# A decoder layer on one core: context keys transposed in DRAM and split on GpSimd, a new order of the attention loop, expert numbers unpacked with explicit register instructions

## The reference, cut to what matters

```python
x = x + attn(layernorm(x))            # 16 heads of 16, 4 key/value groups, RoPE, causal, window 64 + 4 sink tokens
x = x + xattn(layernorm(x), ctx, ctx) # 16 heads, causal; queries, keys and values are used as they are, no projection
x = x + moe(layernorm(x))             # 16 experts of width 176, top 4 per token, and a shared one of width 704
# xattn: scores = einsum('bhqd,bhkd->bhqk', q, k) / 4, causal mask, softmax, times v
# moe:   coef of the 4 best softmaxed gate logits; h = silu(g) * u; y = h @ w2[e].T, added up with coef
```

## Time and profile before

| | us |
|---|---|
| median of 3 runs | 416.64 |
| lowest, highest | 412.84, 417.04 |
| the profiled execution, as timed | 414.46 |
| its span, first to last instruction | 412.6 |
| busy: PE, weight loads, DVE, ACT, POOL | 364.2, 260.7, 254.8, 180.3, 157.5 |
| mean granted clock of TensorE | 0.960 |

### The profile page before, as it was taken

One profiled execution on the slowest core, in us unless ns is written; L12 is line 12 of the kernel. 1 busy time (PEld: TensorE's weight loads), 2 busy tenths in 40 slices (PEclk: granted clock), 3 DMA queues, 4 the chain that ended last, 5 costly groups with the idle time before them and its releaser, 6 DMA issues.

```text
span 412.6 us, 7763 instructions
## 1 busy us (share of the span) xinstructions
PE 364.2 (88%) x2198; PEld 260.7 (63%) x2198; DVE 254.8 (62%) x744; ACT 180.3 (44%) x538; POOL 157.5 (38%) x203
## 2 busy tenths in 40 slices
PE   7687998989899895986997949999999999999883
PEld 3345675757586864755866725666666666668662
DVE  2647799797979689876254633444444444443894
ACT  1052867676758476674424312333333333332220
POOL 2923416262625324566537500333333333333000
PEclk9898999999989999999798978999999999999997
DMA  7990000878676671111102143667666666662901
GB/s 237 350 387 2 2 1 2 249 221 255 202 251 207 213 247 39 41 67 52 54 26 94 66 143 93 195 191 206 192 202 201 186 208 198 193 195 98 390 24 51
DMA packets 43029, 64.25 MB, mean 156 GB/s; under 512 B 5251, under 2 KB 31892, under 8 KB 42484
## 3 DMA queue, kind: packets, MB, share of 16 engines
q1 hardware_dynamic: 38356, 52.45, 41.0%
q0 software_dynamic: 3792, 10.49, 6.7%
q10 hardware_dynamic: 848, 0.92, 0.9%
HBM read 34.88 MB, written 28.97 MB: 155 GB/s over the span
## 4 chain that ended last, share of the span: by engine, by line
PE 38%; issue 24%; DVE 16%; POOL 13%; ACT 4%; DMA 3%; SPq 1%; POOLq 0%; DVEq 0%
POOL y_picks L595 11%; PE bank L1414 10%; PE bank L1328 5%; PE bank L1343 5%; ACT probs L637 3%; PE bank L1319 3%; DVE neg_max L874 3%; PE bank L1283 3%; PE bank L1314 2%; DVE x L1243 2%; PE bank L1370 2%; PE bank L1302 2%; DVE q_stk L846 1%; PE bank L1397 1%; PE bank L1384 1%
## 5 line engine op out<-in xcount | busy, mean ns | idle before, releaser
L595 POOL DMA_INDIRECT y_picks<-yb,ids x47 | 45.1, 959 | 93.7 <-DVE yb L1215 93.1
L637 ACT ACTIVATE probs<-bank,neg_max 128x128 f32<-128x128 f32 x256 | 69.9, 414 | 16.0 <-DVE neg_max L874 16.0
L1669 PE MATMUL bank<-w,xbt 128*128 x188 | 69.2, 492 | 1.0 <-ACT xbt L764 0.8
L1208 DVE TENSOR_TENSOR hb<-sg,bank 128x176 f32<-128x176 f32 x47 | 15.9, 338 | 67.8 <-issue 23.8
L772 ACT ACTIVATE sg<-bank 128x176 f32<-128x176 f32 x47 | 14.9, 317 | 84.7 <-PE bank L1669 84.7
L1669 PEld LDWEIGHTS bank<-w,xbt 128*128 128x128 f32 x188 | 32.7, 193 | 26.9 <-issue 17.3
L1689 PE MATMUL bank<-w,hbt 128*128 128x256 f32 x188 | 48.2, 380 | 0.0
L874 DVE TENSOR_REDUCE neg_max<-bank 128x4 f32<-128x512 f32 x64 | 41.0, 683 | 11.3 <-PE bank L1319 11.3
L539 POOL DMA_INDIRECT x_slots<-x,slots x32 | 32.8, 1025 | 23.1 <-DVE slots L1003 14.2
L1328 PE MATMUL bank<-ident,probs 128*128 128x128 f32 x256 | 36.6, 282 | 2.1 <-ACT probs L637 2.1
L880 DVE COPY probs_t<-bank 128x512 f32<-128x512 f32 x47 | 31.9, 685 | 7.5 <-PE bank L1328 7.3
(11 more groups left out here) (176 smaller groups left out, 717.0 us busy)
## 6 DMA issues: line engine op xcount, KB each, us to landing
x_slots<-zero_b SPq DMA_DIRECT2D x16, 1056.0 KB, 10.6
w<-w_in_dram SPq DMA_DIRECT2D x47, 256.0 KB
xb<-x_slots SPq DMA_DIRECT2D x47, 132.0 KB, 2.4
w<-w_in_dram SPq DMA_DIRECT2D x4, 1408.0 KB, 10.8
yg<-y_picks SPq DMA_DIRECT2D x8, 512.0 KB, 7.0
sw_raw<-shared_in_dram SPq DMA_DIRECT2D x6, 384.0 KB, 3.5
ctx_sb<-ctx_in_dram SPq DMA_DIRECT2D x1, 1024.0 KB, 12.0
out_dram<-x SPq DMA_DIRECT2D x8, 128.0 KB, 1.8
```

What stands on the lines that cost most here:

```text
L595: pool.indirect_dma_start(y_picks[:, :], bass.IndirectOffsetOnAxis(ids[:, n:n + 1], 0), yb[:, n % RB, :], None).then_inc(yb_placed[n % RB] ...
L637: ins = act.activation(probs[:, g, j, :], ps_s[g][:, 128 * j:128 * j + 128], ACT.Exp, bias=neg_max[:, g, j:j + 1])
L1669: ins = pe.matmul(ps_gu[n % 2][:, 0:GU], xbt[:, n % 2, k, :], w13[:, bass.ds(e, 1), k, :].rearrange("p e n -> p (e n)"), start=k == 0, sto ...
```

## The change

The host lays the context out a second time, with the channel on the partitions: per sequence 128 partitions of 2 x 4 x 128 values, each head's 16 channels written three times and a block of zeros, in the order of the stack. SP loads it, sequence by sequence (512 KB), into `ctxt`. POOL's `split_keys` rounds all of it into `ktc` and then overwrites partitions 32 to 63 and 96 to 127, which hold the low parts and the zeros, with the difference. `stack_context`, `cross_keys` and `cross_k` are gone, and with them `c_stk`, `ctx_rows` and a memset.

The stacks of keys and queries change places: context keys become (high, high, low, 0), context queries (high, low, high, 0).

All four engines' `iteration` is in a new order, `row_max`, `exps` and `transpose_probs` are now called bank by bank, and ACT takes banks 2 and 3 where it took 2. `unpack` writes its two register instructions out.

```diff
@@ SP
+            def load_keys(c):
+                if c:
+                    sp.wait_ge(ktc_ready, 2 * c)
+                sp.dma_start(ctxt[:, :, :, :].rearrange("p u j n -> p (u j n)"), ctxt_in[c]).then_inc(ctxt_loaded, 16)
+            load_keys(0)
+            load_keys(1)
+            load_keys(2)
             sp.wait_ge(zeros_ready, 1)
             for c in range(1, SC):
                 sp.wait_ge(swl_ready, c)
 ...
+                load_keys(c + 2)
@@ POOL
+            def split_keys(c):
+                pool.wait_ge(ctxt_loaded, 16 * c + 16)
+                if not isinstance(c, int) or c:
+                    pool.wait_ge(scores_psum[CROSS], 4 * c)
+                if not isinstance(c, int) or c:
+                    pad_context(c - 1)
+                pool.tensor_copy(ktc[:, :, :, :], ctxt[:, :, :, :]).then_inc(ktc_high, 1)
+                pool.wait_ge(ktc_high, c + 1)
+                for low in (slice(PAD, STK), slice(STK + PAD, 2 * STK)):
+                    pool.tensor_tensor(ktc[low, :, :, :], ctxt[low, :, :, :], ktc[low, :, :, :].bitcast(F32), ALU.subtract
+                                       ).then_inc(ktc_ready, 1)
+                pool.wait_ge(ktc_ready, 2 * c + 2)
             def iteration(t, cross_on, tail_on):
-                if cross_on:
-                    pad_context(t - 1)
+                if tail_on:
+                    split_shared(t - 2)
                 turn(t + 1)
                 if tail_on:
                     inverse_deviation(CROSS, t - 2)
-                stack_context(t)
 ...
+                split_keys(t)
                 if tail_on:
                     keep_rows(t - 2)
-                    split_shared(t - 2)
                 inverse_deviation(SELF, t)
@@ POOL behind the loop, the new order
+            split_shared(SC - 1); inverse_deviation(CROSS, B - 3); split_keys(B - 1); keep_rows(B - 3)
+            inverse_deviation(SELF, B - 1); scatter(0); pad_context(B - 1); inverse_deviation(CROSS, B - 2)
+            keep_rows(B - 2); scatter(1); scatter(2); scatter(3)
@@ PE, iteration, the new order (conditions left out)
+   scores(SELF, t, 0); front_a(t + 1); scores(SELF, t, 1); logits(lot); front_b(t + 1)
+   transpose_probs(SELF, t, 0); transpose_probs(SELF, t, 1); cross_queries(c, 0); turn_values(CROSS, t - 2)
+   transpose_probs(SELF, t, 2); transpose_probs(SELF, t, 3)
+   wait ktc_ready, qtc_ready, probs_t_ready; scores(CROSS, c, 0); cross_queries(c, 1)
+   values(SELF, t, 0); values(SELF, t, 1); scores(CROSS, c, 1); third_norm(t - 2)
+   transpose_probs(CROSS, c, 0); turn_values(SELF, t); transpose_probs(CROSS, c, 1); front_c(t + 1, 0)
+   transpose_probs(CROSS, c, 2); turn_attn(t); transpose_probs(CROSS, c, 3); front_c(t + 1, 1)
+   project(t); values(CROSS, c, 0); values(CROSS, c, 1); ranks(lot)
@@ ACT, iteration, the new order
+   take_values(CROSS, t - 2); front_a(t + 1); exps(SELF, t, 0..3); route_exps(lot); cross_q(c, 0)
+   take_probs_t(SELF, t, 2); take_probs_t(SELF, t, 3); cross_q(c, 1); exps(CROSS, c, 0); take_values(SELF, t)
+   exps(CROSS, c, 1); take_xth(t - 2); exps(CROSS, c, 2); exps(CROSS, c, 3); front_c(t + 1, 0); take_attn_t(t)
+   take_probs_t(CROSS, c, 2); take_probs_t(CROSS, c, 3); front_c(t + 1, 1)
@@ DVE, iteration, the new order
+   second_norm(c); stack_queries(c); row_max(SELF, t, 0..3); route_slots(0) if last; route_shift(lot); front_r(t + 1)
+   first_norms (iterations 0 and 1); take_probs_t(SELF, t, 0); take_probs_t(SELF, t, 1); cross_rows(t - 2)
+   statistics(CROSS, t - 2); row_max(CROSS, c, 0); row_max(CROSS, c, 1); front_p(t + 1); third_norm(t - 2)
+   row_max(CROSS, c, 2); front_l(t + 1); row_max(CROSS, c, 3); take_xtl(t - 2); route_top(lot); normalise(SELF, t)
+   take_probs_t(CROSS, c, 0); front_k(t + 1); take_probs_t(CROSS, c, 1); front_v(t + 1); route_pick(lot)
+   front_n(t + 2); x2 of t; statistics(SELF, t)
@@ PE, expert numbers
             def unpack(n):
-                experts[n] = pe.snap((packed[n // PACK] >> (4 * (n % PACK))) & (NE - 1), min_val=0, max_val=NE - 1)
+                r = pe.alloc_register(f"expert{n}")
+                pe.reg_alu(r, packed[n // PACK], 4 * (n % PACK), ALU.logical_shift_right)
+                pe.reg_alu(r, r, NE - 1, ALU.bitwise_and)
+                experts[n] = pe.snap(r, min_val=0, max_val=NE - 1)
```

More of the change, by code:

```diff
@@ L562, in _ @@
                 iteration(t, True, True)
-            pad_context(B - 2)
+            split_shared(SC - 1)
+            inverse_deviation(CROSS, B - 3)
+            split_keys(B - 1)
+            keep_rows(B - 3)
+            inverse_deviation(SELF, B - 1)
             pool.wait_ge(rows_zeroed, 16 * (NE + 1))
@@ L568, in _ @@
             scatter(0)
[L569 to L573, removed]
             pad_context(B - 1)
-            scatter(2)
             inverse_deviation(CROSS, B - 2)
             keep_rows(B - 2)
+            scatter(1)
+            scatter(2)
             scatter(3)
-            split_shared(SC - 1)
             pool.wait_ge(xn3_kept, B - 1)
@@ L675, in iteration @@
                     take_values(CROSS, t - 2)
+                if not last:
+                    front_a(t + 1)
+                for g in range(TILES):
+                    exps(SELF, t, g)
                 if lot is not None:
                     route_exps(lot)
-                exps(SELF, t, 0)
-                if not last:
-                    front_a(t + 1)
                 if cross_on:
-                    cross_k(t - 1, 0)
                     cross_q(t - 1, 0)
-                exps(SELF, t, 1)
+                take_probs_t(SELF, t, 2)
+                take_probs_t(SELF, t, 3)
                 if cross_on:
-                    cross_k(t - 1, 1)
                     cross_q(t - 1, 1)
-                take_probs_t(SELF, t, 2)
+                    exps(CROSS, t - 1, 0)
                 take_values(SELF, t)
                 if cross_on:
-                    exps(CROSS, t - 1, 0)
+                    exps(CROSS, t - 1, 1)
                 if tail_on:
@@ L1049, in iteration @@
                     front_v(t + 1)
-                if cross_on:
-                    take_probs_t(CROSS, t - 1, 3)
                 if lot is not None:
                     route_pick(lot)
-                if not tail_on:
-                    dve.wait_ge(x_rest, 16)
-                    first_norms(LATER[t])
+                if isinstance(t, int) and t < B - 2:
+                    dve.wait_ge(rstd1_ready, 2)
+                if not isinstance(t, int) or t < B - 2:
+                    front_n(t + 2)
                 dve.wait_ge(wo_psum, t + 1)
@@ L1491, in iteration @@
                     pe.wait_ge(qtc_ready, 2 * t)
-                    pe.wait_ge(ktc_ready, 2 * t)
-                if cross_on:
                     scores(CROSS, c, 1)
+                if lot is not None:
+                    pe.wait_ge(exps_ready, 2 * lot + 2)
+                if last:
+                    pe.wait_ge(slots_ready, 1)
                 if tail_on:
                     third_norm(t - 2, ps_x)
+                if cross_on:
+                    transpose_probs(CROSS, c, 0)
                 turn_values(SELF, t)
+                if cross_on:
+                    transpose_probs(CROSS, c, 1)
                 if not last:
@@ L1501, in iteration @@
                 if cross_on:
[L1502 removed]
+                    transpose_probs(CROSS, c, 2)
                 if tail_on:
@@ L1507, in iteration @@
                 if cross_on:
-                    transpose_probs(CROSS, c, 1)
-                project(t)
-                if lot is not None:
-                    ranks(lot)
+                    transpose_probs(CROSS, c, 3)
                 if not last:
                     front_c(t + 1, 1)
+                project(t)
                 if cross_on:
@@ L1516, in iteration @@
                     values(CROSS, c, 1)
+                if lot is not None:
+                    ranks(lot)
             def count_experts():
@@ L1613, in _ @@
             rows_of(0)
-            transpose_probs(CROSS, B - 1, 0)
-            transpose_probs(CROSS, B - 1, 1)
+            for g in range(TILES):
+                transpose_probs(CROSS, B - 1, g)
             pe.wait_ge(attn_ready[CROSS], B - 1)
```

181 lines of the change are left out of this document (73 added, 108 removed).

## The result

| | before | after |
|---|---|---|
| median, lowest, highest us | 416.84, 412.84, 417.33 | 429.70, 428.41, 430.25 |
| ratio, 95% interval | | 1.0326, 1.0257 to 1.0394 |
| span of the profiled execution | 412.6 | 428.4 |
| mean granted clock | 0.960 | 0.919 |

A forecast was written before the change was run, and what follows sets the result against it. PE and DVE were taken to bound the attention loop together, PE's sequencer the expert loop. Attention -8.9 and experts -8.2 us, together -17.1, take the profiled 414.46 to 397.4; with the median 2.2 above, 399, range 391 to 408.

The forecast's parts named there:

- Expert numbers: Expert loop: shift and mask run under the up matmuls instead of behind a wait; beat 2.50 us, -8.2 us in all.
- POOL's prices: Attention loop, `split_keys` on POOL: cast up to 1.36 us, each subtraction 2.37, whole block with `pad_context` and gaps 7.1.
- the first rival: POOL gates the attention loop; at a block of 9.2 us its gain is gone, about 406 us; chance 0.18.
- the slower rival: POOL's block takes 11.5 us or more, with subtractions of 4.6; beat 23.1, kernel 423 us; chance 0.06.
- the walk through one iteration: One steady attention iteration timed piece by piece from the end of `project`; beat from 20.76 to about 19.2 us.
- stacking 0.85, with POOL now busy beside it 0.4 more: DVE after `second_norm`: stacking takes 0.85 us plus 0.4 for POOL beside it, reaching `row_max(SELF)` at 4.2.
- `front_l` 15.5 (1.34, POOL beside it): DVE after `row_max(CROSS,2)`: `front_l` takes 1.34 us beside POOL and ends at 15.5 us of the iteration.
- the forecast beat: Attention loop: plain beat of about 19.2 us instead of 20.76, -1.55, with POOL nearly co-bound.
- Iterations 6 and 7: Attention loop's end: iteration 6 gains 2.5 us, with PE's mask wait covered; iteration 7 gains half a beat's gain, 0.7.
- The tail: Behind the attention loop: no gain at `scatter(0)`, and `split_keys(7)` may end 0.5 us after the statistics; +0.5 us.
- The start: Iterations 0 and 1: priced at 0, though `split_keys(0)` waits for 512 KB more behind the first loads.
- The wait for the key load that the prediction named at its end: POOL waiting for the key load, named as something that would make the prediction wrong; priced at nothing.

The follow-up runs named there:

- e6: Changed kernel with `front_l(t + 1)` ahead of `row_max(CROSS, t - 1, 2)` on DVE; 410.18 us, ratio 0.9859 to the kernel before.
- e9: e6 with the second norm and `stack_queries` behind the first two SELF row maxima on DVE; 403.36 us, ratio 0.9649 to the kernel before.
- e11: Changed kernel with eight unread matmuls on zeros per beat where PE waits for `k_stk`; 426.38 us, ratio 1.0262 to the kernel before.
- e5: Changed kernel with POOL's `split_shared(t - 2)` moved behind `inverse_deviation(CROSS, t - 2)`; 427.22 us, ratio 1.031 to the kernel before.
- e7: Changed kernel with both the DVE exchange of e6 and the POOL move of e5; 430.25 us, ratio 1.0382 to the kernel before.
- e10: e9 with eight unread matmuls on zeros in iteration 7 and eight in the tail; 404.01 us, ratio 0.9714 to the kernel before.
- e1: Kernel before with only the new `unpack` of the expert numbers; 404.33 us, ratio 0.9749 to the kernel before.
- e4: Changed kernel with both POOL key subtractions cut to 8 columns, so the keys' low part is left out; 407.04 us, ratio 0.9798 to the kernel before.
- e12: e9 with `load_keys(0)` issued on SP ahead of the four loads of `w13`; 405.02 us, ratio 0.9716 to the kernel before.

## Why the prediction was wrong

*Expert numbers: right.* Beat 2.50 in nearly every block, 8.2 us, no ALU_OP at the matmul's line.

*POOL's prices: right.* A subtraction of 1,024 columns on 32 partitions takes 2.37 us, as the slope of rows on 128 partitions gave, so the number of partitions doesn't count; the cast takes 1.04 instead of 1.36, the block 6.3 instead of 7.1. POOL is idle 3.58 us before `rstd`: it doesn't gate the beat, as forecast and against the first rival. At the shorter beats of e6 and e9 this sign turns: there POOL has no idle time before that `rstd`, which starts 0.3 us behind the end of DVE's `ve`. In e6 DVE waits 1.0 us for it (0.8 in after), in e9 it has two row maxima to do first. So POOL is near its limit there, as the prediction said. In the slower rival the place was near, but the mechanism (POOL's subtraction at 4.6 us) was not it.

*The failed step* is the walk through one iteration, at two of its terms: "stacking 0.85, with POOL now busy beside it 0.4 more" and "`front_l` 15.5 (1.34, POOL beside it)". I read the spread of 0.22 to 0.84 us of the earlier trace rows as two engines that slow each other a little. It was a wait for the end of POOL's instruction, and short because the POOL instructions then beside it were short (the earlier trace rows has 0.40 to 1.82, the long one elsewhere). The change makes them 1.82 and 2 x 2.37 long and puts them beside DVE's SBUF work. Measured: +1.67 for the cast instead of +0.4, and for `front_l` 0.87 and 2.14 on top, 3.6 us in all instead of 1.34. The trace of before showed it already. In its timelines of iteration 3 the 0.84 us of `k_stk` end 0.08 us behind a cast of POOL's:

```profile
91.37 0.84 DVE L857 TENSOR_TENSOR k_stk<-qk,k_stk 128x64 fp32r<-128x64 f32 x1
```

```profile
91.11 1.02 POOL L525 CAST sw_h<-sw_raw 128x768 f32 x1
```

The Trainium skill, "SBUF — State Buffer", section "Who interferes with whom", says that VectorE in a two-port mode, which casts and copies can take, and GpSimd hold the ports that they share as an exclusive lock for a whole instruction while the other "fully blocks", and that a VectorE instruction with two SBUF inputs contends with a GpSimd instruction that reads SBUF. By that rule an instruction of DVE's of either kind costs up to the whole of POOL's. The trace agrees: the cast takes 2.09 beside 1.82, the subtraction 2.36 beside 2.37. The prediction cited only that the ports are shared.

*What stands behind the waiting instruction* I walked, but with the small terms. The differences between kernels price it: from after to e11 1.0 us a beat (24.0 to 23.0: the clock), from e11 to e6 2.4 (to 20.6: q and k stacked under the keys' split), from e6 to e9 1.7 (to 18.9: the cast with all four row maxima of SELF behind it). Together 5.1, and what is left is the forecast beat. These are steps in one order, and they don't simply add in another: e5, whose `qc_stk` cast is free, takes 2.5 us off three of after's four beats, though the stacking of k takes 1.6 us longer in it, and e7 adds 2.0 to 3.3 to e6's beats by the same move.

*Iterations 6 and 7:* forecast -2.5 and -0.7, measured +3.0 and +2.9. In e9 they are 27.6 (at a clock of 0.82, 1.00 before) and 19.4, still not below 26.5 and 18.9, so there the gains were overrated apart from the lock. *The tail:* forecast +0.5, measured +3.5, and 3.1 in e9. PE stands idle there for 4.9 us instead of 3.1, and its clock is 0.71 instead of 0.83; but e10 filled idle time without a shorter tail, and e1, with the old order, has a tail 1.5 us longer than before. What makes it longer is not settled.

*The start*, priced at nothing: +4.7. In after POOL waits 4.4 us for the keys and then splits them for 6 us ahead of sequence 0's `rstd`, for which DVE waits 2.9 us. e6, with no lock on `k_stk` in iteration 1, has the values of sequence 0 at 56.3; e4, without the long subtractions, has that `rstd` 4.5 us earlier and the values at 52.9, ahead of before's 55.4; e12 takes 3.6 off e9 by the earlier load. The wait for the key load that the prediction named at its end was real, but in e12 its removal came to nothing in the total.

*Net.* Keys and order at their best here (e9, 0.9649, 0.9541 to 0.9756) can't be told from the unpacking alone (e1, 0.9749, 0.9707 to 0.979). Their profiles say where the gain goes: e9 gains 7.4 us in four beats over e1 and loses 4.7 at the start, 1.1 and 0.5 in iterations 6 and 7, 1.6 in the tail and 2.2 behind it. But e9's profile is of an execution 5 us longer than its three shortest (400.2 to 400.9, against 403.8 to 406.3 of e1 on another chip), and in which part those are shorter no trace shows.

## What to carry to other kernels

Before moving work to GpSimd, list which VectorE instructions, reading and writing SBUF alone, can meet it, and price each meeting at up to GpSimd's whole instruction plus everything queued behind the VectorE one. Put VectorE's PSUM reads beside GpSimd's long instructions, and its SBUF work in the gaps; cutting the long instructions helps only where they can't be kept apart. A small register computation ahead of an address on TensorE's queue belongs under a running matmul, not behind a wait.

## What the runs showed of the hardware

- A VectorE instruction of 0.22 us that reads and writes SBUF took 2.36 beside a GpSimd subtraction of 2.37, and 0.41 beside pieces of 256 columns; PSUM reads of 0.68 us kept their time.
- A GpSimd subtraction of 1,024 columns takes 2.37 us on 32 partitions; one of 8 columns 0.19 (e4).
- After an idle wait of TensorE of 2.5 us came 3.4 us at 1.2 GHz, worth 1.0 us of the beat; with matmuls on zeros in the wait none came (e11).
- Moving one 1.82 us instruction on GpSimd's queue cost 20 us (e6 to e7), and exchanging two calls on VectorE's gave 19.5 (after to e6): in this loop of in-order queues with such a lock, order was worth more than work.
